# Masking the first attention's scores on VectorE instead of TensorE in a two-layer kernel

## The chip, the cores and the metric

The kernel runs on one core of a Trainium2 chip. The metric is the device time of one execution in microseconds (us), given as the median of the runs. A core has TensorE (PE) for matmuls, VectorE (DVE), ScalarE (ACT) and GpSimd (POOL) for elementwise work, and SyncE (SP), which issues DMAs here. Each engine runs its own instructions in the order of the program; between engines semaphores keep the order. SBUF is the large on-chip memory, PSUM the small one into which PE writes its results.

## The reference

Two layers, each an attention and a feed-forward part, each with a layer norm in front and behind and a residual sum. The change touches the first attention alone: latent attention over 1024 tokens with 32 heads and a causal mask.

```python
qf = jnp.concatenate([q_nope, q_pe], axis=-1)
kf = jnp.concatenate([k_nope, jnp.broadcast_to(k_pe, (b, H, s, ROPE))], axis=-1)
scores = jnp.einsum('bhqd,bhkd->bhqk', qf, kf) * scale
causal = jnp.tril(jnp.ones((s, s), dtype=bool))
scores = jnp.where(causal, scores, jnp.finfo(scores.dtype).min)
probs = jax.nn.softmax(scores, axis=-1)
o = jnp.einsum('bhqk,bhkd->bhqd', probs, v)
```

## The kernel before

The kernel runs stage after stage: `front` (projections and rotary parts), `mla_heads` (the first attention's heads, the only function that the change touches), `mla_output`, the feed-forward part, then the second attention (`mha_heads`) and the end. The order of the work inside `mla_heads` is written out by hand in loops, one for each engine.

The 32 heads are taken in 16 pairs (`i`). A pair has 16 slots, `s = 2t + e`: `t` is the tile of 128 queries (0 to 7), `e` the head of the pair. Because of the causal mask, slot `s` needs only the first `(t + 1) * 128` keys, so its width grows from 128 to 1024 columns. Scores and probabilities have the queries as partitions and the keys as columns. For each slot:

- `scores` (PE, L770 to L786): three matmuls for each piece of up to 512 columns (L780, L781, L782: high and low parts in float32r) are summed up in one of two PSUM tiles `score_ps[s % 2]`. On the last 128 columns, the diagonal block, a fourth matmul (L784) adds the mask: `ident_bf` (identity, bfloat16) times `mask` (0 below the diagonal, -1e30 above it, bfloat16). It carries the semaphore `scores_ready`.
- `take_max` (DVE, L966 to L971): `reduce_max` over the slot's columns, negated, into `minus_max`; it carries `max_ready`.
- `exp` (ACT, L887 to L896): `exp(score + minus_max)` into `probs` with the sum of each row; the trace shows the read of that sum as an instruction of its own, ACTIVATION_READ_ACCUMULATOR. `probs_ready` follows, which frees the score tile for slot s + 2.
- `turn` (PE, L788 to L800): the probabilities are transposed block by block into two PSUM tiles, the first four blocks by L794 and the others by L799. In the upper slots (`s >= 8`) both are used in each slot; the first waits for the semaphore `dve_turned`, the second for `act_turned`, of the slot before.
- `take_turned`: the copies out of these tiles, by DVE for the first (L979, in lower slots L983) and by ACT for the second (L904, L908).
- `mix_low` and `mix_high` (PE, L808 and L820): the product with the latent values, once for the lower four tiles and once for the upper four of each pair.

PE's order is: small preparations of later pairs (L744 to L768), a part of the last pair's `mix_high` or this pair's `mix_low` at some slots, then `scores` of slot s + 2, then `turn` of slot s. DVE's order is `take_max` of slot s + 1, then `take_turned` of slot s - 1, then now and then the low parts of the preparations (L949, L955, L963), the inverses of the sums (L989) and the product of the mix with them (L996). ACT's order is `exp` of slot s, then its copy of slot s - 1, then its share of the preparations. SP issues the loads of weights and rotary parts, a round trip of the inverses through memory, and the stores of the mix. POOL makes low parts of the rotary queries.

At the start of the stage DVE casts mask and identity to bfloat16 (L943, L944). PE waits for both before its first matmul of the stage, which also waits for the weights.

Of the kernel before, what the change touches and what calls it, by code (L numbers as in the profile page):

```python
# [19 lines left out]
BF16 = mybir.dt.bfloat16  # L20
I32 = mybir.dt.int32
ALU = mybir.AluOpType
ACT = mybir.ActivationFunctionType
AX = mybir.AxisListType

P = 128
S = 1024
# [32 lines left out]
def wait(engine, semaphore, value):  # L60

    if isinstance(value, int) and value <= 0:
        return
    engine.wait_ge(semaphore, value)
# [540 lines left out]
def mla_heads(nc, io, ident, m, h, pe_scratch, r_scratch, a_scratch):  # L605

    sem = Semaphores(nc, "mh")
    with ExitStack() as ctx:
        sb = lambda n, s, d=F32: ctx.enter_context(nc.sbuf_tensor(f"mh_{n}", s, d))
# [10 lines left out]
        q_hi, q_lo = (part[:].rearrange("p (i e) n -> p i e n", i=2) for part in h)  # L620
        probs = sb("probs", [P, 2, S])
        minus_max = sb("minus_max", [P, 4])
# [1 line left out]
        row_inverse = sb("row_inverse", [8, 2, P])  # L624
        spread = sb("spread", [P, BANK])
        mixed = sb("mixed", [P, BANK])
        mask, ident_bf = sb("mask", [P, P], BF16), sb("ident_bf", [P, P], BF16)
        score_ps = [ctx.enter_context(nc.psum_tensor(f"mh_score{i}", [P, S], F32)) for i in range(2)]
        turn_ps = [ctx.enter_context(nc.psum_tensor(f"mh_turn{i}", [P, 4, P], F32)) for i in range(2)]
        mix_ps = ctx.enter_context(nc.psum_tensor("mh_mix", [P, BANK], F32))  # L630
# [1 line left out]
        consts, zeroed = sem("consts"), sem("zeroed")  # L632
# [4 lines left out]
        scores_ready, max_ready, probs_ready = sem("scores_ready"), sem("max_ready"), sem("probs_ready")  # L637
# [8 lines left out]
        def groups_before(i, s):  # L646

            return 24 * i + (s if s < 8 else 8 + 2 * (s - 8))
# [9 lines left out]
        def absorb_at(i):  # L658

            return (-1, 0) if i == 0 else (0, 1) if i == 1 else (0, 9) if i == 2 else (i - 2, 6)  # L660
# [20 lines left out]
        def rows_of(e):  # L681

            return slice(e * CR, (e + 1) * CR), slice((1 - e) * CR, (2 - e) * CR)
# [55 lines left out]
        def _(pe):  # L739
# [30 lines left out]
            def scores(i, s):  # L770
                t, e = divmod(s, 2)
                if s == 0 or s == 8:
                    pe.wait_ge(prep_used, queries_no(i, s // 8) + 1)
                    pe.wait_ge(pe_lo_ready, 4 * i + 2 + s // 4)
                wait(pe, probs_ready, SLOTS * i + s - 1)
                q = slice(t * P, (t + 1) * P)
                for k0, k1, base in score_pieces(t):
                    out, k = score_ps[s % 2][:, base + k0:base + k1], slice(k0, k1)
                    diagonal = k1 == (t + 1) * P
                    nc.tensor.matmul(out, q_hi[:, i % 2, e, q], m["kt_hi"][e][:, k], start=True, stop=False)  # L780
                    nc.tensor.matmul(out, q_hi[:, i % 2, e, q], m["kt_lo"][e][:, k], start=False, stop=False)  # L781
                    last = nc.tensor.matmul(out, q_lo[:, i % 2, e, q], m["kt_hi"][e][:, k], start=False, stop=not diagonal)  # L782
                    if diagonal:
                        last = nc.tensor.matmul(score_ps[s % 2][:, base + k1 - P:base + k1], ident_bf[:], mask[:],  # L784
                                                start=False, stop=True)
                last.then_inc(scores_ready, 1)  # L786

            def turn(i, s):  # L788
# [71 lines left out]
        @block.scalar  # L860
        def _(act):
            def take_absorbed(i):
                act.wait_ge(prep_ready, absorb_no(i) + 1)
                nc.scalar.copy(absorbed_hi[:].rearrange("p a n -> p (a n)"), prep_ps[:, 0:2 * P]).then_inc(absorbed_ready, 1)

            def take_output(i):
                act.wait_ge(prep_ready, output_no(i) + 1)
                nc.scalar.mul(w_hi[:, i, :], prep_ps[:], m["kw2"][:, 0:1]).then_inc(w_out_ready, 1)

            def take_queries(i, half):  # L870
                act.wait_ge(prep_ready, queries_no(i, half) + 1)
                for e in range(2):
                    rows = rows_of(e)[0]
                    last = nc.scalar.copy(q_hi[rows, i % 2, e, half_of(half)], prep_ps[rows, :])
                last.then_inc(q_hi_ready, 1)

            def take_rotary(i, e):
                act.wait_ge(pe_in, 16 * (i + 1))
                rows = rows_of(e)[1]
                nc.scalar.copy(q_hi[rows, i % 2, e, :], pe32[rows, :]).then_inc(pe_hi_ready, 1)  # L880

            def take_rows(i, half):
                act.wait_ge(prep_ready, row_no(i, half) + 1)
                wait(act, row_out, 16 * (2 * (i - 1) + half + 1))
                nc.scalar.copy(row_inverse[:, half, :], prep_ps[0:8, 0:P]).then_inc(prep_used, 1)

            def exp(i, s):  # L887
                t, e = divmod(s, 2)
                n = SLOTS * i + s
                act.wait_ge(max_ready, n + 1)  # L890
                if n >= 2:
                    act.wait_ge(turns_ready, groups_before(i, s - 1) if s else groups_before(i, 0) - 2)
                base, width = score_pieces(t)[0][2], (t + 1) * P
                nc.scalar.activation(probs[:, s % 2, 0:width], score_ps[s % 2][:, base:base + width], ACT.Exp,  # L894
                                     bias=minus_max[:, s % 4:s % 4 + 1],
                                     accum_out=sums[:, i % 2, t // 4, 4 * e + t % 4:4 * e + t % 4 + 1]).then_inc(probs_ready, 1)  # L896

            def take_turned(i, s):
                t, e = divmod(s, 2)
                q = slice(t % 4 * P, (t % 4 + 1) * P)  # L900
                if s >= 8:
                    act.wait_ge(turns_ready, groups_before(i, s) + 2)
                    wait(act, mix_ready, 2 * i)
                    nc.scalar.copy(high_turned[:, 4:t + 1, e, q], turn_ps[1][:, 0:t - 3, :]).then_inc(act_turned, 1)  # L904
                elif e == 1:
                    act.wait_ge(turns_ready, groups_before(i, s) + 1)
                    wait(act, mix_ready, 2 * i - 1)
                    nc.scalar.copy(low_turned[:, 0:t + 1, e, q], turn_ps[1][:, 0:t + 1, :]).then_inc(act_turned, 1)  # L908

            take_absorbed(0)  # L910
            take_rotary(0, 0)
            take_rotary(0, 1)
            take_output(0)
            take_queries(0, 0)
            take_queries(0, 1)
            for i in range(PAIRS):
                for s in range(SLOTS):
                    exp(i, s)
                    if s:
                        take_turned(i, s - 1)  # L920
                    elif i:
                        take_turned(i - 1, SLOTS - 1)
                    for ahead in range(3):
                        if i + ahead < PAIRS:
                            if absorb_at(i + ahead) == (i, s - 1):
                                take_absorbed(i + ahead)
                            if output_at(i + ahead) == (i, s - 1):
                                take_output(i + ahead)
                            for half in range(2):
                                if queries_at(i + ahead, half) == (i, s - 1):  # L930
                                    take_queries(i + ahead, half)
                    if i and row_at(i - 1, 1) == (i, s - 1):
                        take_rows(i - 1, 1)
                    if row_at(i, 0) == (i, s - 1):
                        take_rows(i, 0)
                    if i < LAST and s in (2, 3):
                        take_rotary(i + 1, s - 2)
            take_turned(LAST, SLOTS - 1)
            take_rows(LAST, 1)

        @block.vector
        def _(dve):
            nc.vector.tensor_copy(mask[:], m["mask"][:]).then_inc(consts, 1)  # L943
            nc.vector.tensor_copy(ident_bf[:], ident[:]).then_inc(consts, 1)  # L944

            def lower_absorbed(i):
                dve.wait_ge(absorbed_ready, i + 1)
# [18 lines left out]
            def take_max(i, s):  # L966
                t = s // 2
                dve.wait_ge(scores_ready, SLOTS * i + s + 1)
                base, width = score_pieces(t)[0][2], (t + 1) * P
                nc.vector.reduce_max(minus_max[:, s % 4:s % 4 + 1], score_ps[s % 2][:, base:base + width], AX.X, negate=True  # L970
                                     ).then_inc(max_ready, 1)  # L971

            def take_turned(i, s):
                t, e = divmod(s, 2)
# [74 lines left out]
def score_pieces(t):  # L1049


    n = (t + 1) * P
    if n <= BANK:
        return [(0, n, 0)]
    if n == BANK + P:
        return [(0, BANK - P, P), (BANK - P, n, P)]
    return [(0, BANK, 0), (BANK, n, 0)]
# [1000 lines left out]
```

## Time and profile before

| | |
|---|---|
| time, median of 3 runs | 1638.69 us (1638.67 to 1639.95) |
| the profiled execution's own time | 1633.25 us |
| its span | 1631.4 us |
| TensorE busy | 1512.2 us, 93% |
| VectorE busy | 1031.7 us, 63% |
| ScalarE busy | 810.1 us, 50% |

The profile is of one execution. Busy times are unions over an engine's instructions; TensorE's matmuls are pipelined and their ends are modelled, so that two of them overlap in the rows, and the price of one is read from start to start. Weight loads are kept apart (PEld) and overlap the matmuls. "Idle before, releaser" names what an engine waited for ahead of a group of instructions, as far as the profile can tell from the semaphores. L784 is line 784 of the kernel.

### The profile page before, as it was taken

How to read it: one execution, taken by the hardware profiler on the slowest of the kernel's cores; microseconds unless marked ns; L12 is line 12 of the kernel's file. 1: busy time of each engine (PE TensorE's matmuls, PEld its weight loads, DVE VectorE, ACT ScalarE, POOL GpSimd, SP SyncE). 2: the span in 40 equal slices, each digit the busy share in tenths (PEclk: the TensorE clock that was granted, in tenths of full speed). 3: DMA queues.
4: the chain of work that ended last, by engine and by line, in shares of the span. 5: the costliest groups of instructions: out<-in, count | busy, mean ns of one | idle time of the engine just before them, and what ended most of it. 6: DMA issues, size and time to landing. Idle time of an engine off the chain costs nothing. (4 is left out here: it accounts for less than half of the span.)

```text
span 1631.4 us, 22633 instructions
## 1 busy us (share of the span) xinstructions
PE 1512.2 (93%) x8286; PEld 990.9 (61%) x8286; DVE 1031.7 (63%) x1792; ACT 810.1 (50%) x1467; POOL 232.1 (14%) x233
## 2 busy tenths in 40 slices
PE   6867999999999999987979999898999999999986
PEld 4645676766667776656868888787553333333254
DVE  5744666666666666644553433465889999999345
ACT  5325666666666666642212222222207777777834
POOL 2752111111111111100000000001000133331200
PEclk9977999999999999998989999999999999999998
DMA  4142221212112211124321120106730232320001
GB/s 136 52 190 71 85 69 63 69 62 68 63 62 82 85 69 40 34 85 153 103 78 59 58 78 20 52 1 174 188 46 8 69 75 79 79 67 15 18 14 46
DMA packets 63298, 116.84 MB, mean 72 GB/s; under 512 B 12830, under 2 KB 32414, under 8 KB 61902
## 3 DMA queue, kind: packets, MB, share of 16 engines
q1 hardware_dynamic: 59956, 106.63, 20.7%
q10 hardware_dynamic: 3168, 8.65, 2.1%
q8 instruction: 67, 1.10, 0.3%
q14 instruction: 43, 0.35, 0.1%
q0 software_dynamic: 64, 0.11, 0.0%
HBM read 83.04 MB, written 29.66 MB: 69 GB/s over the span
## 5 line engine op out<-in xcount | busy, mean ns | idle before, releaser
L1683 DVE TENSOR_REDUCE ah_minus_half<-ah_ring 128x1 f32<-128x512 f32 x512 | 319.7, 679 | 36.6 <-PE ah_ring L1580 35.8
L970 DVE TENSOR_REDUCE mh_minus_max<-mh_score 128x1 f32<-128x128 f32 (+7 forms) x256 | 193.5, 756 | 196.4 <-PE mh_score L784 196.1
L1643 ACT ACTIVATE ah_probs<-ah_score 128x1024 f32<-128x1024 f32 x256 | 248.7, 1023 | 109.7 <-PE ah_score L1597 108.9
L894 ACT ACTIVATE mh_probs<-mh_score,mh_minus_max 128x128 f32<-128x128 f32 (+7 forms) x256 | 189.8, 742 | 35.6 <-DVE mh_minus_max L970 33.3
L1580 PE MATMUL ah_ring<-ah_k_stack,ah_q_stack 48*128 48x512 f32 x512 | 184.3, 461 | 15.3 <-DMA ah_k_stack<-qk_scratch 5.9
L1580 PEld LDWEIGHTS ah_ring<-ah_k_stack,ah_q_stack 48*128 48x128 f32 x512 | 81.5, 187 | 176.2 <-DVE ah_minus_half L1683 160.4
L1597 PE MATMUL ah_score<-ah_q_stack,ah_k_stack 49*128 49x512 f32 x512 | 155.3, 439 | 3.9 <-DVE ah_v L1707 2.3
L780 PE MATMUL mh_score<-shared,h_hi 128*128 128x512 f32 (+3 forms) x384 | 151.2, 394 | 2.4 <-ACT mh_probs L894 2.4
L1043 POOL TENSOR_TENSOR h_lo<-mh_pe,h_hi 64x512 fp32r<-64x512 f32 x64 | 81.8, 1278 | 469.9 <-ACT h_hi L880 466.3
L1612 PE MATMUL ah_mix<-ah_probs,ah_v 128*32 128x512 f32 x1024 | 137.2, 608 | 0.6 <-ACT ah_probs L1643 0.6
L782 PE MATMUL mh_score<-shared,h_lo 128*128 128x512 f32 (+3 forms) x384 | 131.7, 343 | 0.0
L781 PE MATMUL mh_score<-shared,h_hi 128*128 128x512 f32 (+3 forms) x384 | 131.4, 342 | 0.0
L794 PE MATMUL mh_turn<-ident,mh_probs 128*128 128x128 f32 x672 | 107.4, 277 | 2.5 <-DVE mh_high_turned L979 0.4
L780 PEld LDWEIGHTS mh_score<-shared,h_hi 128*128 128x128 f32 x384 | 72.9, 190 | 60.0 <-ACT mh_probs L894 35.0
L904 ACT COPY mh_high_turned<-mh_turn 128x128 f32<-128x128 f32 (+3 forms) x128 | 54.6, 427 | 103.5 <-PE mh_turn L799 103.5
L820 PE MATMUL mh_mix<-mh_high_turned,ck 128*64 128x512 f32 (+3 forms) x512 | 102.9, 524 | 0.0
L979 DVE COPY mh_high_turned<-mh_turn 128x512 f32<-128x512 f32 x128 | 87.3, 682 | 4.6 <-PE mh_turn L794 3.9
L1597 PEld LDWEIGHTS ah_score<-ah_q_stack,ah_k_stack 49*128 49x128 f32 x512 | 76.0, 187 | 22.4 <-ACT ah_probs L1643 15.5
L1190 ACT ACTIVATE x<-ff_gate 128x512 f32<-128x512 f32 x28 | 16.7, 598 | 136.9 <-PE ff_gate L1169 136.9
L799 PE MATMUL mh_turn<-ident,mh_probs 128*128 128x128 f32 x480 | 84.4, 274 | 0.0
L1216 DVE TENSOR_TENSOR d<-x,ff_up 128x512 f32<-128x512 f32 x28 | 19.3, 688 | 102.7 <-PE ff_up L1169 102.7
L1963 PE MATMUL n_py<-down_hi,shared 128*128 128x512 f32 x224 | 72.5, 400 | 4.9 <-DVE shared L1956 4.9
(223 smaller groups left out, 2893.0 us busy)
## 6 DMA issues: line engine op xcount, KB each, us to landing
mh_w<-in_w_pairs SPq DMA_DIRECT2D x16, 896.0 KB, 5.5
x<-in_w_inner SPq DMA_DIRECT2D x14, 768.0 KB, 4.2
pe_scratch<-fr_pe_out SPq DMA_DIRECT2D x4, 2048.0 KB, 6.6
mh_pe<-pe_scratch SPq DMA_DIRECT2D x16, 512.0 KB, 4.0
mh_spread<-inverse_scratch SPq DMA_DIRECT2D x64, 128.0 KB, 2.9
a_scratch<-mh_mixed SPq DMA_DIRECT2D x32, 256.0 KB, 2.3
x<-a_scratch SPq DMA_DIRECT2D x8, 1024.0 KB, 5.8
qk_scratch<-ai_ring SPq DMA_DIRECT2D x32, 256.0 KB, 3.6
```

Of the source, the lines that this page charges most:

```text
L780: nc.tensor.matmul(out, q_hi[:, i % 2, e, q], m["kt_hi"][e][:, k], start=True, stop=False)
L781: nc.tensor.matmul(out, q_hi[:, i % 2, e, q], m["kt_lo"][e][:, k], start=False, stop=False)
L782: last = nc.tensor.matmul(out, q_lo[:, i % 2, e, q], m["kt_hi"][e][:, k], start=False, stop=not diagonal)
L794: last = nc.tensor.transpose(turn_ps[0][:, j, :], probs[:, s % 2, j * P:(j + 1) * P], ident[:])
L820: last = nc.tensor.matmul(mix_ps[e * CR:(e + 1) * CR, q0:BANK], m["ck"][:, j, 0:CR], high_turned[:, j, e, q0:BANK], start=j == 0, stop=j = ...
L894: nc.scalar.activation(probs[:, s % 2, 0:width], score_ps[s % 2][:, base:base + width], ACT.Exp, bias=minus_max[:, s % 4:s % 4 + 1], accum ...
L970: nc.vector.reduce_max(minus_max[:, s % 4:s % 4 + 1], score_ps[s % 2][:, base:base + width], AX.X, negate=True).then_inc(max_ready, 1)
L1580: return nc.tensor.matmul(ring[:, m % 3, :], q_stack[a][stack_rows(p, PARTS), c, t * P:(t + 1) * P], k_stack[a][stack_rows(p, PARTS), c, h ...
L1597: last = nc.tensor.matmul(score_ps[c][:, p, :], k_stack[a][rows, c, j * P:(j + 1) * P], q_stack[a][rows, c, half * BANK:(half + 1) * BANK] ...
L1612: last = nc.tensor.matmul(mix_ps[rows, :], v[j][:, 4 * g * 2 * HD + 32 * head:4 * g * 2 * HD + 32 * head + 32], probs[:, 2 * (u % 2) + c, ...
L1643: nc.scalar.activation(probs[:, 2 * (u % 2) + c, :], score_ps[c][:].rearrange("p e n -> p (e n)"), ACT.Exp, scale=MHA_SCALE).then_inc(prob ...
L1683: nc.vector.reduce_max(minus_half[:, m:m + 1], ring[:, m % 3, :], AX.X, negate=True).then_inc(max_taken, 1)
```

## The change

The mask's matmul goes, and the third product (L782) closes each group and signals. The mask becomes a tile of 128 x 1024 in bfloat16: 896 columns of zero, then the diagonal block. Slot s takes its last `width` columns, so the block lies on the slot's diagonal. `take_max` is one `tensor_tensor_reduce` on VectorE: it writes -(score + mask) back into the PSUM tile of the scores for all `width` columns, and the minimum of these values, which is the negated maximum, into `minus_max`. The exponential reads the negated scores and multiplies them by -1. The identity in bfloat16 is gone; at the start a memset of the 896 columns and one cast take the place of two casts.

```diff
-        mask, ident_bf = sb("mask", [P, P], BF16), sb("ident_bf", [P, P], BF16)
+        mask = sb("mask", [P, S], BF16)
...
-                    diagonal = k1 == (t + 1) * P
                     nc.tensor.matmul(out, q_hi[:, i % 2, e, q], m["kt_hi"][e][:, k], start=True, stop=False)
                     nc.tensor.matmul(out, q_hi[:, i % 2, e, q], m["kt_lo"][e][:, k], start=False, stop=False)
-                    last = nc.tensor.matmul(out, q_lo[:, i % 2, e, q], m["kt_hi"][e][:, k], start=False, stop=not diagonal)
-                    if diagonal:
-                        last = nc.tensor.matmul(score_ps[s % 2][:, base + k1 - P:base + k1], ident_bf[:], mask[:],
-                                                start=False, stop=True)
+                    last = nc.tensor.matmul(out, q_lo[:, i % 2, e, q], m["kt_hi"][e][:, k], start=False, stop=True)
...
-                                     bias=minus_max[:, s % 4:s % 4 + 1],
+                                     bias=minus_max[:, s % 4:s % 4 + 1], scale=-1.0,
...
-            nc.vector.tensor_copy(mask[:], m["mask"][:]).then_inc(consts, 1)
-            nc.vector.tensor_copy(ident_bf[:], ident[:]).then_inc(consts, 1)
+            nc.vector.memset(mask[:, 0:S - P], 0.0).then_inc(consts, 1)
+            nc.vector.tensor_copy(mask[:, S - P:S], m["mask"][:]).then_inc(consts, 1)
+            dve.wait_ge(consts, 2)
...
-                nc.vector.reduce_max(minus_max[:, s % 4:s % 4 + 1], score_ps[s % 2][:, base:base + width], AX.X, negate=True
-                                     ).then_inc(max_ready, 1)
+                scores = score_ps[s % 2][:, base:base + width]
+                nc.vector.tensor_tensor_reduce(out=scores, in0=scores, in1=mask[:, S - width:S], scale=-1.0, scalar=3e38, op0=ALU.add,
+                                               op1=ALU.min, accum_out=minus_max[:, s % 4:s % 4 + 1]).then_inc(max_ready, 1)
```

## Rows read from the trace of the kernel before

**Rows 1.** The page's first part: each engine's busy us, share and instructions.
```profile
PE 1512.2 (93%) x8286; PEld 990.9 (61%) x8286; DVE 1031.7 (63%) x1792; ACT 810.1 (50%) x1467; POOL 232.1 (14%) x233
```

**Rows 2.** Changed stage: length, busy PE, PEld, DVE, ACT, POOL, clock, DMA share, GB/s.
```profile
132.00:720.00 588.00, 579.18 (x3655) 407.37 (x3655) 376.66 (x616) 367.33 (x857) 76.71 (x60) 0.99 0.19 63
```

**Rows 3.** Timeline around a pair's end: start, us, engine, line, op, tiles, shape, count, [idle].
```profile
431.86 0.29 DVE L970 TENSOR_REDUCE mh_minus_max<-mh_score 128x1 f32<-128x128 f32 x1 [1.81 <-PE mh_score L784]
...
432.31 0.69 DVE L979 COPY mh_high_turned<-mh_turn 128x512 f32<-128x512 f32 x1 [0.15 <-PE mh_turn L794]
...
432.83 0.23 PE L784 MATMUL mh_score<-mh_mask,mh_ident_bf 128*128 128x128 bf16 x1
...
433.14 0.63 PE L794 MATMUL mh_turn<-ident,mh_probs 128*128 128x128 f32 x4
...
468.55 0.29 DVE L970 TENSOR_REDUCE mh_minus_max<-mh_score 128x1 f32<-128x128 f32 x1 [1.80 <-PE mh_score L784]
```

**Rows 4.** Timeline, slots 11 to 14 of that pair, DVE and PE.
```profile
458.50 1.09 DVE L970 TENSOR_REDUCE mh_minus_max<-mh_score 128x1 f32<-128x896 f32 x1 [0.27 <-PE mh_score L784]
...
459.51 0.68 DVE L979 COPY mh_high_turned<-mh_turn 128x512 f32<-128x512 f32 x1
...
460.30 0.23 PE L784 MATMUL mh_score<-mh_mask,mh_ident_bf 128*128 128x128 bf16 x1
...
460.37 0.60 PE L794 MATMUL mh_turn<-ident,mh_probs 128*128 128x128 f32 x4
460.57 1.09 DVE L970 TENSOR_REDUCE mh_minus_max<-mh_score 128x1 f32<-128x896 f32 x1 [0.38 <-PE mh_score L784]
...
462.69 1.23 DVE L970 TENSOR_REDUCE mh_minus_max<-mh_score 128x1 f32<-128x1024 f32 x1 [0.44 <-PE mh_score L784]
```

**Rows 5.** Groups by line: engine, op, tiles, shapes, count, busy us, mean ns, idle before.
```profile
L784 PE MATMUL mh_score<-mh_mask,mh_ident_bf 128*128 128x128 bf16 x256 | 59.1, 231 | 0.0
...
L894 ACT ACTIVATION_READ_ACCUMULATOR mh_probs<-mh_score,mh_minus_max 128x1 f32 x256 | 49.9, 195 | 0.0
```

**Rows 6.** Timeline, slots 9 and 10 of that pair, DVE and PE.
```profile
454.56 0.96 DVE L970 TENSOR_REDUCE mh_minus_max<-mh_score 128x1 f32<-128x768 f32 x1 [1.24 <-PE mh_score L784]
...
455.43 0.68 DVE L979 COPY mh_high_turned<-mh_turn 128x512 f32<-128x512 f32 x1
...
455.97 0.23 PE L784 MATMUL mh_score<-mh_mask,mh_ident_bf 128*128 128x128 bf16 x1
456.03 0.74 DVE L955 SCALAR_TENSOR_TENSOR w_vo_lo<-mh_prep,kw,w_vo_hi 128x512 fp32r<-128x512 f32 x1
...
456.26 0.63 PE L794 MATMUL mh_turn<-ident,mh_probs 128*128 128x128 f32 x4
...
456.69 0.94 DVE L970 TENSOR_REDUCE mh_minus_max<-mh_score 128x1 f32<-128x768 f32 x1
...
457.55 0.68 DVE L979 COPY mh_high_turned<-mh_turn 128x512 f32<-128x512 f32 x1
...
458.24 0.23 PE L784 MATMUL mh_score<-mh_mask,mh_ident_bf 128*128 128x128 bf16 x1
...
458.38 0.63 PE L794 MATMUL mh_turn<-ident,mh_probs 128*128 128x128 f32 x4
```

**Rows 7.** Groups of DVE by line and shape, whole run, columns as rows 5.
```profile
L970 DVE TENSOR_REDUCE mh_minus_max<-mh_score 128x1 f32<-128x1024 f32 x32 | 39.2, 1225 | 14.9 <-PE mh_score L784 14.9
...
L996 DVE TENSOR_TENSOR mh_mixed<-mh_mix,mh_spread 128x512 f32<-128x512 f32 x32 | 21.8, 680 | 12.5 <-DMA mh_spread<-inverse_scratch 12.5
...
L989 DVE RECIPROCAL mh_inverse<-mh_sums 128x8 f32<-128x8 f32 x32 | 6.1, 192 | 0.0
...
L222 DVE MEMSET n_eps<- 128x1 f32 x2 | 0.1, 59 | 4.2 <-PEq L79 3.8 <-PEq L1125 0.3
```

**Rows 8.** Timeline at the stage's start: DVE's cast of the mask, PE's first matmul.
```profile
115.33 0.24 DVE L943 CAST mh_mask<-mask 128x128 bf16<-128x128 f32 x1 [11.36 <-PEq L79]
...
120.08 0.66 PE L744 MATMUL mh_prep<-mh_w 128*128 128x64 f32 x2 [13.14 <-DMA mh_w<-in_w_pairs]
```

## The prediction

> **What bounds the kernel now.** First the page's sums, then the stretches: TensorE (PE) is busy for 93% of the span [rows 1]. The changed code runs from about 120 to 720 us, in its steady state from 132. There PE is busy 579.18 of 588 us at a granted clock of 0.99, VectorE (DVE) 376.66 and ScalarE (ACT) 367.33 [rows 2]. So the stage belongs to PE, and DVE has 36% of its time free. But a busy share of matmuls with modelled ends hides short waits, so I read starts next.
>
> One pair of heads takes 468.55 - 431.86 = 36.69 us, sixteen of them 587 us [rows 3]. Inside a pair I look at what stands between the start of a mask matmul (L784) and the next PE matmul. Mostly it is 0.06 or 0.07 us, as 460.30 to 460.37 [rows 4]; the 0.23 us that the group of L784 gives as a mean [rows 5] is latency and not the price. In two of the 16 slots it is about 0.3 us: 432.83 to 433.14 [rows 3] and 455.97 to 456.26 [rows 6], and once 0.14 (458.24 to 458.38) [rows 6]. There PE waits for DVE to empty the PSUM tile of the turned probabilities.
>
> **Removed from PE.** Per pair 16 mask matmuls at 0.066 us (middle of the 0.06 and 0.07 above) = 1.06 us, over 16 pairs 16.9 us. This is the most that can be gained, unless the step from one operand type to the other costs a little too; the trace has no scores matmul directly followed by a turn, so I leave 0.01 us for each (2.6 us) to the range.
>
> **What does not come back.** Two places give nothing or less.
> First, slot 15's turn at 433.14 waits for the copy of slot 14 (432.31 + 0.69 = 433.00, and 0.14 until PE starts) [rows 3], which follows turn 14 and not a mask. The mask in front of it (432.83) only shortens time in which PE waits anyway: minus 0.07 us of gain per pair.
> Second, the upper slots of a pair hang on DVE. DVE does the maximum of slot s+1, then the copy of slot s-1, and turn s waits for that copy. For slot 9: maximum 10 starts at 454.56, its copy at 455.43, which ends at 456.11, and the turn starts at 456.26, 0.15 later [rows 6]. For slot 10 DVE runs through maximum 10, the copy, L955, maximum 11 and another copy without idling, ending at 457.55 + 0.68 = 458.23, and the turn starts at 458.38 [rows 6]. For slot 11 the copy ends at 459.51 + 0.68 = 460.19, ready for PE at 460.34, where PE's own work starts the turn at 460.37 [rows 4]: 0.03 us of slack. Slots 12 and 13 look the same. So from slot 9 on, the two engines are tied, and what the maximum costs more is paid in time.
>
> **The new maximum.** Call d what the new instruction takes longer than the old, from start to the moment its result counts. Let me follow one pair. Eight masks (slots 2 to 9) lie ahead of the point where scores 10 end; PE runs there with DVE waiting for it, so 8 x 0.066 = 0.53 us come back. Maximum 10 also starts one mask earlier relative to its scores: 0.06. It then delays by d: turn 9 gains 0.59 - d. Turn 10 has two maxima of the same unbroken DVE run ahead of it: 0.59 - 2d. From there PE wins 0.066 a slot by its own work and DVE loses d each second slot (turn 12 hangs on scores 13, which follow turn 10): turn 11 gains 0.65 - 2d, turn 12 0.72 - 3d, turn 13 0.77 - 3d; the scores behind it add one mask more, and turn 15 none. Per pair 0.84 - 3d, over 16 pairs **13.4 - 48d us**.
>
> How large is d? No row of before shows this instruction, nor any DVE instruction that writes PSUM. For the streaming part: the old maximum takes 1.225 us for 1024 elements and 0.29 for 128, so 1.04 ns an element [rows 3, 7], and the tensor-tensor operation with one input in PSUM and one in SBUF (L996) takes 680 ns for 512 [rows 7], where the maximum's 0.29 for 128 and 384 more at 1.04 ns make 0.69 us. A second input thus adds nothing. The accumulated minimum may need to be written out on its own, as ScalarE does for its sums: 195 ns for each [rows 5]. DVE's own smallest instructions take 59 ns (MEMSET, 128x1) and 192 ns (RECIPROCAL, 128x8) [rows 7]. DVE starts an instruction some 0.08 us before the one before has ended (copy at 455.43 against a maximum that ends at 454.56 + 0.96 = 455.52) [rows 6], so such a read adds between -0.02 (nothing) and 0.11 us. I take d = 0.07, above the middle of these, since ScalarE's read, the row most like it, is as long as the long one. For a fixed part that is worse than that I allow up to 0.35 us, two such long rows (192 ns) behind one another.
> The Trainium skill bears on this: "VectorE: DVE Perf Modes", section "Two Vector instructions with no wait between them", says that an operation which also writes out its accumulator is two instructions. No row of before shows it on DVE; ScalarE's pairs of rows show it there. With one instruction only, d would be 0 and the gain 13.4 us.
>
> **Sum.** 13.4 - 48 x 0.07 = 10.0 us. ScalarE computes the exponential with another scale in the same instruction, at no cost. At the stage's start the mask's cast (0.24 us at 115.33) and the identity's go, and a MEMSET over 896 columns comes, some 0.93 us at the 1.04 ns an element above; PE needs it only together with the weights, and its first matmul of the stage starts at 120.08 behind that transfer, more than 3 us after [rows 8]. No DMA and no queue is moved; the stages behind start earlier as a whole. The profiled execution took 1633.25 us (span and 1.85 us around it) and would take 1623.2; the median of the runs shown is 1638.69, 5.4 above it, so I forecast 1628.7.
>
> **Rivals.**
> *A, forecast:* d between 0 and 0.15 us. Gain 13.4 down to 6.2 us: 1625.3 to 1632.5. Chance 0.62.
> *B, the fixed part is larger:* d from 0.15 to 0.35. Gain 6.2 down to about -3.4 us: 1632.5 to 1642.1; up to d = 0.21 it still gains over 3.3 us, and over 0.28 it costs a little faster than this line, since a third maximum joins the unbroken run. Chance 0.16.
> *C, half rate, the slower side:* reading and writing the same PSUM bank, or the fused instruction itself, streams at half the rate of the old maximum. Then d is about 1.05 ns x width: 0.81 for 768, 0.94 for 896, 1.07 for 1024. The five maxima from 454.56 on that lie ahead of turn 13 add 2 x 0.81 + 2 x 0.94 + 1.07 = 4.57 us; DVE's idle time among them (0.27, 0.38 and 0.44 before maxima 12 to 14 [rows 4]) takes up 1.09, so turn 13 comes 3.5 us later. Less 0.53 + 0.06 + 0.07 of masks, a pair takes 2.8 us more: +45 us, 1684. It decides from d over 0.28, where 13.4 - 48d turns negative. For it: PSUM as a target of DVE is unseen. Against it: L996 at full rate with PSUM as a source. Chance 0.14.
> The page "Vector Engine (DVE) Microarchitecture Reference", section "Points that are easy to get wrong", of the Trainium skill states that the scalar-tensor-tensor form halves its throughput with two SBUF sources that are not bf16. By it this edit escapes C, as one source is in PSUM and the other is bf16; no run here shows the other case.
> *D, the whole gain and more:* the mask's going also shortens the step to the turns, d is 0: 13.4 + 2.6 = 16.0 us, 1622.7. Chance 0.08.
>
> **How the numbers follow.** A measurement of this kernel can tell about 0.2%, 3.3 us, from no change. Faster by more: A, D and 0.05 of B, 0.75, less 0.04 for waits in the lower slots that the rows don't show: 0.71. Same: those 0.04 and 0.07 of B: 0.11. Slower: C and the last 0.04 of B: 0.18. The range is A, D and all of B but its last part, which leaves out 0.18: 1622 to 1641.
>
> **What would show it.** In the profile after: no L784; the maxima's group with its 1024-column form at 1225 ns plus d or followed by DVE's 256 reads of an accumulator; a pair in 36.69 - 0.6 = 36.1 us; the turns of slots 9 to 13 all starting 0.15 us behind the end of a copy; all stages behind 720 us unchanged in length. The forecast is wrong if the 1024-column instruction takes over 1.5 us, or if the lower slots, which I take as PE's, turn out to wait for DVE.

## The result and the profile after

The changed kernel takes 1623.24 us (median of 8 runs, 1617.21 to 1626.15); the one before takes 1635.59 us in the 8 runs that go with them (1630.22 to 1639.95). The ratio is 0.9916, 95% interval 0.9897 to 0.9934. Timed again later beside the kernel before (e9): 0.9937, interval 0.9916 to 0.9959. So it is faster by some 0.75%, about 12 us, while single runs of one kernel spread over up to 12.5 us (1629.59 to 1642.05 in the later runs of the kernel before). Still no run of the changed kernel reached any of the kernel before: its longest took 1627.58 us. The trace is finer: inside the changed stage the steady pairs of heads all take 35.84 to 35.89 us.

First the page and the stretches of the changed kernel, and the stretch behind the stage in the kernel before:

```profile
PE 1502.8 (93%) x8030; PEld 991.4 (61%) x8030; DVE 1038.6 (64%) x2048; ACT 810.8 (50%) x1467; POOL 232.0 (14%) x233
```
Stretches: start:end, length, busy PE, PEld, DVE, ACT, POOL, granted clock, DMA share, GB/s; changed kernel:
```profile
132.00:707.50 575.50, 563.67 (x3398) 404.22 (x3396) 381.94 (x872) 368.20 (x857) 76.83 (x60) 0.99 0.20 64
707.50:1624.20 916.70, 847.29 (x4199) 519.81 (x4199) 581.48 (x1019) 393.48 (x484) 85.38 (x91) 0.96 0.23 69
```
The kernel before, behind its stage:
```profile
720.00:1631.40 911.40, 841.12 (x4199) 516.52 (x4199) 580.08 (x1019) 393.37 (x484) 85.48 (x91) 0.96 0.24 69
```
TensorE has 256 instructions fewer, VectorE 256 more, with 7 us more of busy time. From its first maximum to its last the stage is 12.1 us shorter (136.59 to 703.04 us instead of 136.89 to 715.48).

Behind it nothing was changed, and yet the profiled execution needs some 5 us more there, for the same 4199 matmuls. From the last maximum to the end it is 916 us in the profile of before, 921 in that of the changed kernel, and 916 to 924 in the eleven traces of the experiments below, whichever kernel stands ahead. The shortest and the longest of these, e3_upper and e8, read as the stretches above:
```profile
705.38:1621.04 915.66, 844.39 (x4230) 518.50 (x4230) 583.53 (x1024) 395.77 (x489) 85.42 (x91) 0.96 0.24 69
```
```profile
697.71:1621.82 924.11, 852.24 (x4230) 522.67 (x4228) 584.58 (x1023) 395.81 (x489) 85.35 (x91) 0.96 0.24 68
```
TensorE is busy 7.9 us longer with the same 4230 matmuls, and that is most of the 8.4 us. The granted clock of the whole execution goes the same way: 0.967 in the first and 0.960 in the second, 0.966 in the profile of before and 0.961 in that of the changed kernel. The later runs of the kernel before agree: three at a clock of 0.961 took 1638.61 to 1642.05 us, the one at 0.968 took 1629.59. So the spans of two profiles (7.2 us apart here) say less about this edit than the stage does.

Inside the stage the granted clock is 1.00 from the second pair of heads on, and lower in the first alone: 0.91 before and 0.88 in the changed kernel. That first pair got 0.23 us longer (38.29 us instead of 38.06), while the later ones got some 0.82 shorter. In e1 below, where the first pair has 0.91 as before, it got 0.51 shorter (37.55). The stretch that begins with the scores of slot 11 of this pair, changed kernel, then kernel before:
```profile
159.10:162.00 2.90, 2.90 (x15) 2.61 (x13) 1.54 (x4) 0.99 (x2) 0.00 (x0) 0.54 0.00 0
```
```profile
160.30:163.30 3.00, 3.00 (x21) 2.56 (x19) 2.39 (x5) 1.99 (x5) 0.00 (x0) 1.00 0.00 0
```
Here the changed kernel has a granted clock of 0.54 behind a wait of 1.66 us, and its 512-column matmuls start 0.43 us apart; the kernel before has 1.00 behind a wait of 1.58, and they start 0.23 apart. Why the one fell and the other did not, no run here settles.

The end of a steady pair, changed kernel (timeline; answers [rows 3]):
```profile
425.99 0.30 DVE L968 CUSTOM_DVE_ANT_0 mh_score<-mh_score,mh_mask 128x128 f32<-128x128 f32 x1 [1.74 <-PE mh_score L781]
...
426.45 0.69 DVE L977 COPY mh_high_turned<-mh_turn 128x512 f32<-128x512 f32 x1
...
426.87 0.27 PE L781 MATMUL mh_score<-shared,h_lo 128*128 128x128 f32 x1
...
427.29 0.63 PE L790 MATMUL mh_turn<-ident,mh_probs 128*128 128x128 f32 x4 [0.15 <-DVE mh_high_turned L977]
...
461.89 0.30 DVE L968 CUSTOM_DVE_ANT_0 mh_score<-mh_score,mh_mask 128x128 f32<-128x128 f32 x1 [1.75 <-PE mh_score L781]
```
A pair is 461.89 - 425.99 = 35.90 us here, 35.87 as the median of eleven steady pairs, against 36.69 before: 0.82 us less. Turn 15 still starts 0.15 us behind the end of the copy of slot 14 (426.45 + 0.69 = 427.14), as before; the trace now names that wait.

Slots 9 and 10, changed kernel (answers [rows 6]):
```profile
448.11 0.97 DVE L968 CUSTOM_DVE_ANT_0 mh_score<-mh_score,mh_mask 128x768 f32<-128x768 f32 x1 [1.16 <-PE mh_score L781]
...
448.99 0.14 DVE L968 DVE_READ_ACCUMULATOR2_ANT mh_minus_max<- 128x1 f32 x1
448.99 0.69 DVE L977 COPY mh_high_turned<-mh_turn 128x512 f32<-128x512 f32 x1
...
449.39 0.28 PE L781 MATMUL mh_score<-shared,h_lo 128*128 128x256 f32 x1
449.59 0.74 DVE L952 SCALAR_TENSOR_TENSOR w_vo_lo<-mh_prep,kw,w_vo_hi 128x512 fp32r<-128x512 f32 x1
449.82 0.63 PE L790 MATMUL mh_turn<-ident,mh_probs 128*128 128x128 f32 x4 [0.15 <-DVE mh_high_turned L977]
450.25 0.95 DVE L968 CUSTOM_DVE_ANT_0 mh_score<-mh_score,mh_mask 128x768 f32<-128x768 f32 x1
...
451.12 0.68 DVE L977 COPY mh_high_turned<-mh_turn 128x512 f32<-128x512 f32 x1
...
451.60 0.34 PE L781 MATMUL mh_score<-shared,h_lo 128*128 128x384 f32 x1
...
451.96 0.52 PE L790 MATMUL mh_turn<-ident,mh_probs 128*128 128x128 f32 x3
```
The read of the accumulator is there as a row of its own, 0.14 us long, and the copy behind the maximum starts in the same 0.01 us as the read: it doesn't wait for it. From the start of the maximum to the start of the copy it is 0.88 us, where the kernel before had 0.87 [rows 6].

ScalarE's exponential needs the result itself. Where it waits for the maximum it starts later. Kernel before, the exponential behind the maximum at 456.69 [rows 6], then changed kernel, the one behind the maximum at 450.25:
```profile
457.67 0.90 ACT L894 ACTIVATE mh_probs<-mh_score,mh_minus_max 128x768 f32<-128x768 f32 x1 [0.37 <-DVE mh_minus_max L970]
```
```profile
451.30 0.90 ACT L890 ACTIVATE mh_probs<-mh_score,mh_minus_max 128x768 f32<-128x768 f32 x1 [0.44 <-DVE mh_minus_max L968]
```
That is 0.98 us from the start of the maximum before and 1.05 now: the result counts 0.07 us later.

The groups say the same: changed kernel, and the 768-column form of the kernel before last (for 1024 columns see [rows 7]).
```profile
L968 DVE CUSTOM_DVE_ANT_0 mh_score<-mh_score,mh_mask 128x1024 f32<-128x1024 f32 x32 | 39.4, 1233 | 12.7 <-PE mh_score L781 12.7
...
L968 DVE DVE_READ_ACCUMULATOR2_ANT mh_minus_max<- 128x1 f32 x256 | 34.4, 134 | 0.7
L968 DVE CUSTOM_DVE_ANT_0 mh_score<-mh_score,mh_mask 128x768 f32<-128x768 f32 x32 | 30.8, 962 | 16.7 <-PE mh_score L781 16.7
```
```profile
L970 DVE TENSOR_REDUCE mh_minus_max<-mh_score 128x1 f32<-128x768 f32 x32 | 30.5, 952 | 17.1 <-PE mh_score L784 17.0
```
The fused instruction reads a second operand, writes PSUM in place and takes 8 to 10 ns more in each of its eight widths: rival C, half rate, is out.

### The profile page after: what moved, and what is told of

It is laid out like the page before. It is cut to its first block and busy times, and to the rows that moved or that the text cites. A ratio compares the mean times of both kernels' runs of the same rounds, so it can differ in the third digit from the quotient of the medians.

```text
span 1624.2 us, 22378 instructions
## 1 busy us (share of the span) xinstructions
PE 1502.8 (93%) x8030; PEld 991.4 (61%) x8030; DVE 1038.6 (64%) x2048; ACT 810.8 (50%) x1467; POOL 232.0 (14%) x233
## 5 line engine op out<-in xcount | busy, mean ns | idle before, releaser
L968 DVE CUSTOM_DVE_ANT_0 mh_score<-mh_score,mh_mask 128x128 f32<-128x128 f32 (+7 forms) x256 | 195.8, 765 | 179.4 <-PE mh_score L781 179.3
L790 PEld LDWEIGHTS mh_turn<-ident,mh_probs 128*128 128x128 f32 x672 | 76.0, 141 | 26.0 <-issue 21.7
```

The source lines that it names most:

```text
L790: last = nc.tensor.transpose(turn_ps[0][:, j, :], probs[:, s % 2, j * P:(j + 1) * P], ident[:])
L968: nc.vector.tensor_tensor_reduce(out=scores, in0=scores, in1=mask[:, S - width:S], scale=-1.0, scalar=3e38, op0=ALU.add, op1=ALU.min, accu ...
```

## The experiments

Each is read by the length of a steady pair: from the first maximum of one pair to that of the next, as the median of eleven pairs in the trace. Two theories were open. H: the read is hidden on VectorE's queue, so that d, what a maximum costs more, is nearly nothing. P: the read costs 0.06 us each time (that much later it ends), and the matmul's going is worth more than 0.066 us. The experiments e1 to e7 were each executed once, so their whole times are not compared.

| kernel | a steady pair, us |
|---|---|
| before | 36.69 |
| changed | 35.87 |
| e1, mask left out, old maximum | 35.82 |
| e2, new maximum, mask's matmul too | 36.73 |
| e3_lower, small copy in slots 0 to 9 | 36.47 |
| e3_upper, small copy in slots 10 to 15 | 36.13 |
| e4_lower, small maximum in slots 0 to 9 | 35.87 |
| e4_upper, small maximum in slots 10 to 15 | 36.21 |
| e5, low mix split | 35.87 |
| e6, low mix split and output moved | 35.77 |
| e7, output moved | 35.73 |
| e8, output moved and turn 15 filled | 35.47 |
| e9, changed kernel again | 35.85 |

**One part alone: the matmul goes, the old maximum stays.** The kernel before with

```diff
-                    last = nc.tensor.matmul(out, q_lo[...], m["kt_hi"][e][:, k], start=False, stop=not diagonal)
-                    if diagonal:
-                        last = nc.tensor.matmul(..., ident_bf[:], mask[:], start=False, stop=True)
+                    last = nc.tensor.matmul(out, q_lo[...], m["kt_hi"][e][:, k], start=False, stop=True)
```

> The kernel before without the mask's matmul and with the old maximum: the causal mask is left out of the computation, everything else stays. So TensorE has what it has in the changed kernel and VectorE has what it had before. Measured is the length of a steady pair in the trace (before 36.70 us, changed kernel 35.87). Theory H (the accumulator read is hidden): the new maximum costs VectorE's queue almost nothing, so this kernel gains no more than the changed one: a pair of 35.80 to 35.87. Rival P (the read costs its 0.06 us three times a pair, as the formula has it, and the matmul's going is worth more than 0.066 us on TensorE): without the new maximum a pair would be shorter by about 3 x 0.06, 35.65 to 35.72.

Timeline of e1, the first maxima of two pairs:
```profile
425.37 0.29 DVE L966 TENSOR_REDUCE mh_minus_max<-mh_score 128x1 f32<-128x128 f32 x1 [1.78 <-PE mh_score L781]
...
461.19 0.29 DVE L966 TENSOR_REDUCE mh_minus_max<-mh_score 128x1 f32<-128x128 f32 x1 [1.75 <-PE mh_score L781]
```
35.82 us: 0.87 less than before, and only 0.05 less than the changed kernel. The new maximum costs 0.05 us a pair, not 0.18: H, and the pure worth of the matmul's going is 0.87, where the prediction had 0.84.

**The other part alone: the new maximum, with the mask still added by TensorE.** The changed kernel with the four lines of the matmul put back and a `mask` of zeros for VectorE (a separate tile holds the block for TensorE).

> The changed kernel with the mask's matmul put back (the second operand of the new maximum is zero, so the result stays): TensorE as before, VectorE as after. Theory H: a pair of 36.70 to 36.76 us, as before, since the queue loses 0.01 to 0.02 us for each maximum, three of them on the path. Rival P: the read's 0.06 counts three times, less the slack of before in the upper slots (0.03 to 0.09 us): 36.80 to 36.88.

Timeline of e2, the first maxima of two pairs:
```profile
433.21 0.30 DVE L974 CUSTOM_DVE_ANT_0 mh_score<-mh_score,mh_mask 128x128 f32<-128x128 f32 x1 [1.79 <-PE mh_score L785]
...
469.94 0.30 DVE L974 CUSTOM_DVE_ANT_0 mh_score<-mh_score,mh_mask 128x128 f32<-128x128 f32 x1 [1.79 <-PE mh_score L785]
```
36.73 us, 0.04 more than before: H again. Divided by the three maxima that the prediction has on the path, the two differences of medians give 0.017 us (e1) and 0.013 (e2) for one maximum, which is the 0.01 of the rows above and a little more. The second is weak: the pairs of e2 alternate between 36.70 and 36.73 us and those of before between 36.69 and 36.71, so that their means are only some 0.015 apart.

**Which slots are tied to VectorE.** The changed kernel with one small instruction behind the maximum, once in slots 0 to 9 and once in 10 to 15. First a copy:

```diff
                                                op1=ALU.min, accum_out=minus_max[:, s % 4:s % 4 + 1]).then_inc(max_ready, 1)
+                if s < 10:
+                    nc.vector.tensor_copy(extra[s % 4][:], mask[:, 0:64])
```

> The changed kernel with one small VectorE copy (64 bfloat16 columns, its result unused) behind the maximum of slots 0 to 9 of each pair, 160 in all. Call c what it adds to the queue, some 0.1 to 0.15 us. If only the upper slots are tied to VectorE (the prediction's chain), a pair stays at 35.87 us, at most 0.05 more by slot 15's turn. If VectorE's time counts everywhere, a pair grows by 10 c, over 1 us.

> The same small copy behind the maximum of slots 10 to 15 instead, 96 in all. By the prediction's chain three of the six count: a pair grows by 3 c, 0.3 to 0.45 us for c of 0.1 to 0.15, thus 36.2 to 36.3. If VectorE is on no path, nothing; if each maximum counts, 6 c, 0.6 to 0.9.

In the upper slots a pair took 0.26 us more: three times the 0.09 that the copy adds to the queue (0.97 us from the start of a 768-column maximum to the next copy, instead of 0.88). That is under the expected 36.2 to 36.3, because c was taken as 0.1 to 0.15. The lower slots gave 0.59 (0.60 by the medians), which neither expectation had. All of it is lost between the turns of slots 5 and 6. From the trace of e3_lower, all engines:

```profile
440.82 5.36 POOL L1044 TENSOR_TENSOR h_lo<-mh_pe,h_hi 64x512 fp32r<-64x512 f32 x4 [31.11 <-ACT h_hi L877]
...
443.86 1.00 DVE L972 COPY mh_extra<-mh_mask 128x64 bf16<-128x64 bf16 x1
...
444.78 0.55 DVE L984 COPY x<-mh_turn 128x384 f32<-128x384 f32 x1
...
445.25 1.38 DVE L961 TENSOR_TENSOR h_lo<-mh_prep,h_hi 64x512 fp32r<-64x512 f32 x2
...
446.77 0.41 PE L745 MATMUL mh_prep<-mh_w 128*128 128x64 f32 x2 [0.36 <-DVE h_lo L961]
```
While GpSimd (POOL) works, from 440.82 to 446.18, the little copy, which takes 0.18 us elsewhere, takes 1.00. It ends at 444.86, 0.04 us behind the end of the third of GpSimd's four instructions (444.82). There are 30 such long copies in the trace (0.49 or 1.00 us), and each ends 0.04 us behind the end of a GpSimd instruction. The low parts of the queries (L961) come late, and TensorE waits for them ahead of the next preparation: 0.63 us between two matmuls that stand 0.11 apart in the changed kernel, 0.52 of the 0.59. The Trainium skill, "SBUF — State Buffer", section "Who interferes with whom", says that VectorE's copies can run in a mode that takes a port pair shared with GpSimd, and that `tensor_reduce` never does. So the same experiment again with a reduction:

```diff
+                if s < 10:
+                    nc.vector.reduce_max(extra[s % 4][:], mask[:, 0:64], AX.X)
```

> As the experiment with a small copy behind the maxima of slots 0 to 9 (changed kernel), but the small instruction is now a maximum over 64 columns, a form that should not be held up by GpSimd's work. Call c what it adds to the queue, 0.13 to 0.15 us. In the first form all of the 0.59 us that a pair lost stood in one place: the copy behind slot 6's maximum took 1.00 us while GpSimd was at work, and the low parts of the queries came late for the matmul at L744. Theory T (only the upper slots are tied): with c alone the low parts have 0.29 us of slack there, so a pair stays within 0.05 of 35.87 us. Rival (VectorE's time counts in the lower slots): a pair grows by up to 10 c, over 1 us.

> The same small maximum behind the maxima of slots 10 to 15. The small copy there added 0.09 to the queue and a pair 0.26, three times as much. Theory T: again 3 c, 0.39 to 0.45 us, a pair of 36.26 to 36.32. If the tie were something else than the run of maxima and copies, the ratio would change.

e4_lower, 35.85 in this pair and 35.87 as the median; it is the changed kernel's, with ten instructions of 0.21 us more on VectorE:
```profile
424.88 0.30 DVE L969 CUSTOM_DVE_ANT_0 mh_score<-mh_score,mh_mask 128x128 f32<-128x128 f32 x1 [1.73 <-PE mh_score L782]
...
460.73 0.30 DVE L969 CUSTOM_DVE_ANT_0 mh_score<-mh_score,mh_mask 128x128 f32<-128x128 f32 x1 [1.73 <-PE mh_score L782]
```
e4_upper, slot 9:
```profile
448.47 0.97 DVE L969 CUSTOM_DVE_ANT_0 mh_score<-mh_score,mh_mask 128x768 f32<-128x768 f32 x1 [1.16 <-PE mh_score L782]
...
449.35 0.21 DVE L972 TENSOR_REDUCE mh_extra<-mh_mask 128x1 f32<-128x64 bf16 x1
449.48 0.68 DVE L980 COPY mh_high_turned<-mh_turn 128x512 f32<-128x512 f32 x1
...
449.75 0.28 PE L782 MATMUL mh_score<-shared,h_lo 128*128 128x256 f32 x1
...
450.31 0.63 PE L791 MATMUL mh_turn<-ident,mh_probs 128*128 128x128 f32 x4 [0.28 <-DVE mh_high_turned L980]
```
The reduction moves the copy from 0.88 to 1.01 us behind the maximum, c = 0.13, and the turn from 0.43 to 0.56 us behind the last scores matmul. Turns 9, 10 and 12 come 0.13, 0.16 and 0.13 later by themselves, 0.41 in all, of which other turns give a little back: 0.34 us a pair, 2.6 c, a little under the 3 c expected (36.21 us instead of 36.26 to 36.32). The copy's wait for GpSimd was the cause of the 0.59, since with a reduction in its place nothing is lost; that it is a port pair which the two share is what the Trainium skill says in that section; the traces agree and do not show the ports themselves. The chain of the prediction stands: nothing counts in the lower slots, and three of the six maxima in the upper ones.

**Taking the remaining waits away.** First turn 15: two of the four steps of the low mix are issued ahead of it instead of ahead of turn 14.

```diff
                     if s == 14:
-                        mix_low(i)
+                        mix_low(i, 0, 2)
+                    if s == 15:
+                        mix_low(i, 2, 4)
```

> The changed kernel with the low mix of a pair issued in two parts: two of its four steps ahead of turn 14 as before, two ahead of turn 15. If turn 15 only waits for VectorE's copy of slot 14 (0.31 us more from the last scores matmul to the turn than elsewhere in the trace), the moved 0.7 us cover that wait: a pair of 35.54 to 35.60 us, about 5 us in all. Rival: the wait moves to turn 14, which then waits for the copy of slot 13, or to the next pair's first slots, since the product with the mix comes later on VectorE: no gain, 35.85.

Timeline of e5, TensorE:
```profile
457.89 1.72 PE L805 MATMUL mh_mix<-x,ck 128*64 128x512 f32 x8
459.55 0.33 PE L779 MATMUL mh_score<-shared,h_hi 128*128 128x128 f32 x1
...
459.93 0.62 PE L790 MATMUL mh_turn<-ident,mh_probs 128*128 128x128 f32 x4
...
460.92 0.87 PE L805 MATMUL mh_mix<-x,ck 128*64 128x256 f32 x8
...
462.11 0.41 PE L790 MATMUL mh_turn<-ident,mh_probs 128*128 128x128 f32 x2
```
No gain, 35.87, though neither rival explains it: the wait is gone (turn 15 at 462.11 stands 0.11 us behind the last scores matmul, where it was 0.42) and came back nowhere. TensorE itself has 0.33 us more to do: the low mix takes 1.66 + 0.81 us (457.89 to 459.55, 460.92 to 461.73) instead of 2.31 in one piece, and the step from a turn into a mix is 0.20 us where that from a turn into scores is 0.03. Going into this kind of matmul and out of it once more costs as much as the wait.

> The split mix, and the output preparation of a later pair (L752, and with it L952 on VectorE, 0.66 us of its queue) moved from slot 8 to slot 13, with the load of weights issued behind the round trip of the inverses. It takes L952 out of the unbroken run of VectorE ahead of turn 10 (wait of 0.18 there) and fills the tie at turn 13 with TensorE's work: 0.18 to 0.25 less than the split alone, a pair of 35.30 to 35.40. Rival: VectorE is idle or tied elsewhere by as much, or the output's part on ScalarE delays exponential 15: no more than the split alone.

35.77: 0.10 less than the split alone, not 0.18 to 0.25. The move by itself is e7:

```diff
-            return (-1, 1) if i == 0 else (0, 3) if i == 1 else (0, 13) if i == 2 else (i - 2, 8)
+            return (-1, 1) if i == 0 else (0, 3) if i == 1 else (i - 2, 13)
...
+                spread_rows(i, 0)
                 if i + 3 < PAIRS:
                     load_weights(i + 3)
-                spread_rows(i, 0)
```

> The changed kernel with only the output preparation of a later pair moved from slot 8 to slot 13 (no split of the mix). The split alone left a pair at 35.87 us: it took 0.32 us of waiting away and cost TensorE 0.33 for going into the mix a second time; with the move added a pair took 35.77. Turn 10 waits 0.18 us behind an unbroken run of VectorE with L952 in it. If that run is the whole of the move's worth, a pair is 35.70 to 35.78 us; if the split hid a part of it, shorter.

35.73, as expected: 0.14 of the 0.18 us. The trace shows where the rest went: from the last scores matmul to the turn it is 0.18 us less at slot 10 and 0.13 less at slot 9 than in the changed kernel, but 0.17 more at slot 11 (0.35 instead of 0.18), which now waits for VectorE. The last one fills turn 15's wait with work that stands near it anyway, the first two of five matmuls of the next queries' first half (and keeps the move):

```diff
+                    if s == SLOTS - 1 and i + 2 < PAIRS:
+                        prep_queries(i + 2, 0, 0, 2)
```

> The move of the output preparation, and two of the five matmuls of the next queries' first half issued ahead of turn 15, where TensorE waits 0.31 us for VectorE's copy of slot 14; the other three stay where they were. The two take about 0.55 us and need no change between kinds of matmul that was not there. If turn 15's wait hangs on that copy alone, a pair is 0.25 to 0.3 us shorter than with the move: 35.40 to 35.50 us, and the kernel is 18 to 20 us faster than the one before (ratio 0.988 to 0.989). Rival: the wait comes back at the high mix in slot 1, which needs the copies of turn 15: then 35.7, ratio 0.990.

Timeline of e8, TensorE:
```profile
459.81 0.28 PE L784 MATMUL mh_score<-shared,h_lo 128*128 128x128 f32 x1
459.92 0.68 PE L764 MATMUL mh_prep<-shared,mh_absorbed_hi 128*128 128x512 f32 x2
...
460.44 0.60 PE L793 MATMUL mh_turn<-ident,mh_probs 128*128 128x128 f32 x4
```
35.47 us, 0.26 less than with the move: the wait hung on that copy alone. The kernel takes 1617.82 us against 1635.61 before, 17.8 us less, ratio 0.9886, interval 0.9859 to 0.9912. By medians it is 8.2 us under the changed kernel timed beside it, of which the stage accounts for 5.5 to 6 us (560.78 us from first to last maximum instead of 566.26; 0.38 x 16 = 6); the rest is within the scatter. The changed kernel's own measure is the last run:

> The changed kernel itself, timed on the same chip and in the same rounds as the filled one, as its measure: a pair of 35.87 us, ratio to the kernel before 0.990 to 0.993 by the interval that it has; by the stage alone, 12.2 us of 1637, 0.9926.

It came out at 1626.04, ratio 0.9937 (0.9916 to 0.9959), a pair of 35.85. The pair is as expected, the ratio a little above the expected 0.990 to 0.993. The first ratio's interval and this one overlap around the stage's own 0.9926.

## Why the prediction was right or wrong

- **What bounds the stage: right.** TensorE does, and VectorE is tied to it in the upper slots and at turn 15 only. e4_lower (ten instructions more in each pair, no time) and e4_upper show both halves.
- **The price of the mask's matmul: right.** 0.066 us from start to start, 0.84 us a pair after what doesn't come back; e1 measured 0.87. The 0.01 us for a dearer change of operand type, left to the range, is not needed: the difference between 0.87 and 0.84 is 0.03 us over 16 matmuls.
- **Where it does not come back: right.** Turn 15 gave nothing: it now stands 0.42 us behind the last scores matmul, where it stood 0.31 behind the mask's matmul, since TensorE waits through the time that the mask's matmul had filled. How much earlier the turns come, counted from turn 15 of the pair before (means of eleven pairs of either trace): turn 9 0.61 us, turn 10 0.60, turn 11 0.67, turn 12 0.75, turn 13 0.79, turn 14 0.84. The prediction's steps without d are 0.59, 0.59, 0.65, 0.72, 0.77, 0.84. Of the turns of slots 9 to 13, which were all to start 0.15 us behind the end of a copy, four do; turn 11 starts 0.20 behind it.
- **d: the step that failed.** "so such a read adds between -0.02 (nothing) and 0.11 us. I take d = 0.07". As the prediction defines d, up to the moment the result counts, 0.07 is what the exponential shows (0.98 us before, 1.05 now). But the formula charges d to VectorE's queue, three times a pair, and the estimate has the read stand in that queue between the maximum and the next instruction. It does not: the chain needs VectorE's next copy and not the result, and that copy starts beside the read (both at 448.99, the read ending at 448.99 + 0.14 = 449.13). What the queue loses is 0.01 us by the rows and 0.013 to 0.017 by the pairs of e1 and e2, instead of 0.07. With 0.015 the formula gives 0.80 us a pair and 13.4 - 48 x 0.015 = 12.7 in all, where the prediction had 0.63 and 10.0. The steady pairs show 0.82. The whole stage shows 12.1, because the first pair, at a lower clock than before, gained nothing.
- **The forecast time.** 1628.7 us against 1623.24. Of the 5.5 us between them 3.1 are the level: the kernel before has a median of 1635.59 over 8 runs and had 1638.69 in the three that were shown. The other 2.4 are the gain, 12.35 us by the medians instead of 10.0, for which d accounts (48 x 0.055 = 2.6). That the measured time stands next to rival D's 1622.7 is owed to the level and is luck.
- **The other signs.** A pair takes 35.87 us and not 36.1, which is d again. The stages behind were to keep their length; they took 5 us more in the profile, with the granted clock and not with the edit. The MEMSET was to take 0.93 us and took 0.43, and it is on no path: the stage's first matmul starts at 119.70 us, at 120.08 before.
- **Rivals.** A holds: d is between 0 and 0.15 us. B and C are out by d itself. D asked for d = 0 and a dearer change of operand type; for the queue d was nearly so, the other part is not there. The exponential with the other scale takes 741 ns in the mean, 742 before.

## What to carry to other kernels

Before pricing an edit on an engine that is tied to another, ask for each link what the next one needs: the result of the instruction or the engine itself. A small instruction behind a long one can delay the one and not the other. A count of how many copies of the cost lie on the path (three of sixteen here) can be checked by two cheap experiments, the same small instruction put in here and there. Take one that no other engine can hold up: the first probe here waited for GpSimd, and its 0.59 us a pair could be taken for time that counts on VectorE in the lower slots. When work is moved to fill a wait, take a piece that the filling engine can go into and out of at no cost. For an edit under 1%, read the length of a repeated piece inside the trace: here it agreed to 0.02 us between two executions of the changed kernel (35.87 and 35.85), where whole executions differed by several us.

## What the runs showed of the hardware that was not expected

- VectorE's read of the accumulator (134 ns) does not hold up the next instruction of the queue, which starts at the same time (448.99 both). ScalarE, which needs the result, starts 0.07 us later than with the old maximum.
- A 64-column bfloat16 copy between SBUF tiles on VectorE took 0.18 us, and 0.49 and 1.00 us in the two slots in which GpSimd was at work, and all 30 of the long copies ended 0.04 us behind the end of a GpSimd instruction; a reduction over the same columns took 0.21 throughout.
- Splitting a group of fp32 matmuls of 64 rows of output in two cost TensorE 0.33 us, 0.16 inside the parts and 0.17 on the way in.
- The unchanged stages behind took 916 to 924 us in thirteen traces, and TensorE's busy time with the same matmuls differed by 7.9 us between the shortest and the longest, at granted clocks of 0.967 and 0.960 for the whole execution.
